# Attention turned around: 128 rows of x on the partitions, probabilities turned by DMA

## The reference

```python
Sim = (e @ w1)[:, :, None] + (ctx @ w2)[:, None, :] + einsum('bid,bjd->bij', e * w3, ctx) + b
A = softmax(Sim, axis=2);  hq = einsum('bij,bjd->bid', A, ctx)
Batt = softmax(max(Sim, axis=2), axis=1);  hc = einsum('bi,bid->bd', Batt, e)
x = x + tanh(g_x) * (concat([e, hq, e * hq, e * hc]) @ W_qv + b_qv)      # e = layernorm(x)
x = x + tanh(g_f) * top2_of_8_experts(layernorm(x))                      # gelu(x @ w1) @ w2
```

## Time and profile before

| | us |
|---|---|
| time, median of 3 runs (lowest, highest) | 2335.67 (2333.89, 2336.94) |
| time of the profiled execution | 2335.5 |
| its span, first to last instruction | 2333.8 |
| PE busy in the span | 2220.5 (95%) |
| DVE, ACT, POOL busy | 1631.7, 1139.5, 144.6 |
| mean granted clock of PE | 0.985 |

### The profile page before, as it was taken

The page is one execution under the profiler, slowest core; times in us unless marked ns, Lnnn a source line. Parts: engine busy times, 40 slices in busy tenths (PEclk is TensorE's granted clock), DMA queues, the critical chain, the costliest instruction groups (busy, mean ns, idle before and its releaser), DMA issues.

```text
span 2333.8 us, 46974 instructions
## 1 busy us (share of the span) xinstructions
PE 2220.5 (95%) x16817; PEld 1607.4 (69%) x16817; DVE 1631.7 (70%) x3445; ACT 1139.5 (49%) x1607; POOL 144.6 (6%) x143
## 2 busy tenths in 40 slices
PE   5899999999999999999879998599999999999997
PEld 4788888888888888888634544456564655656463
DVE  7688888888888888887856678546554555646450
ACT  6565555544555554555633334336362534546260
POOL 0000000000000000000002222101101010100101
PEclk9999999999999999999999999799999999999999
DMA  7811110011111001101355553333435333333411
GB/s 211 251 28 47 45 45 27 18 45 45 45 45 45 18 27 45 45 27 43 148 200 199 213 184 119 103 104 86 109 124 135 113 99 103 90 103 90 132 61 22
DMA packets 164944, 212.31 MB, mean 91 GB/s; under 512 B 106148, under 2 KB 106276, under 8 KB 156700
## 3 DMA queue, kind: packets, MB, share of 16 engines
q1 hardware_dynamic: 154012, 191.13, 24.9%
q0 software_dynamic: 10880, 20.52, 4.5%
HBM read 123.66 MB, written 71.52 MB: 84 GB/s over the span
## 4 chain that ended last, share of the span: by engine, by line
PE 75%; DVE 13%; ACT 4%; issue 4%; DMA 1%; DVEq 1%; ACTq 0%; POOL 0%; another core or an unknown queue 0%; SPq 0%; POOLq 0%
PE ps L1275 20%; PE ps L1951 18%; PE ps L1966 18%; PE ps L1288 12%; PE ps L1701 5%; DVE arena L828 1%; DVE arena L727 1%; DVE arena L725 1%; ACT arena L1150 1%; DVE arena L822 1%; DVE arena L750 1%; DVE arena L815 1%; DVE arena L734 1%; ACT arena L1147 1%; DVE arena L1530 0%
## 5 line engine op out<-in xcount | busy, mean ns | idle before, releaser
L1275 PE MATMUL ps<-arena 128*128 128x256 f16 x4800 | 555.8, 274 | 25.1 <-DMA arena<-arena 9.9
L1288 PE MATMUL ps<-arena 128*128 (+1 forms) x4864 | 561.0, 273 | 7.3 <-DVE arena L822 7.3
L1275 PEld LDWEIGHTS ps<-arena 128*128 128x128 f16 x4800 | 470.1, 98 | 89.4 <-issue 16.6
L1288 PEld LDWEIGHTS ps<-arena 128*128 128x128 f16 x4864 | 475.2, 98 | 68.0 <-DVE arena L822 7.0
L1951 PE MATMUL ps<-arena 128*128 128x320 f16 x3072 | 421.0, 300 | 17.7 <-DMA arena<-rows 17.7
L1966 PE MATMUL ps<-arena 128*128 128x512 f16 x1920 | 415.7, 379 | 0.0
L1951 PEld LDWEIGHTS ps<-arena 128*128 128x128 f16 x3072 | 301.5, 98 | 136.9 <-issue 17.7
L1966 PEld LDWEIGHTS ps<-arena 128*128 128x128 f16 x1920 | 187.9, 98 | 225.2
L1137 ACT ACTIVATE arena<-ps,arena (+1 forms) x192 | 148.9, 775 | 282.8 <-PE ps L1275 282.8
L1701 PE MATMUL ps<-arena 128*128 128x512 f16 x1080 | 240.4, 380 | 10.6 <-DMA arena<-feats 10.6
L1875 DVE SCALAR_TENSOR_TENSOR arena<-arena 128x640 f16<-128x640 f32 x128 | 113.0, 883 | 136.1 <-ACT arena L1919 136.1
(11 more groups left out here) (249 smaller groups left out, 1821.7 us busy)
## 6 DMA issues: line engine op xcount, KB each, us to landing
arena<-in_L_ffn_w SPq DMA_DIRECT2D x64, 1024.0 KB, 10.0
arena<-feats SPq DMA_DIRECT2D x16, 1536.0 KB
arena<-in_x SPq DMA_DIRECT2D x32, 512.0 KB, 3.9
feats<-arena SPq DMA_DIRECT2D x16, 1024.0 KB, 3.9
rows<-arena SPq DMA_DIRECT2D x1, 10320.0 KB, 32.0
feats<-arena SPq DMA_DIRECT2D x16, 512.0 KB, 3.5
out<-arena SPq DMA_DIRECT2D x16, 512.0 KB, 2.8
arena<-in_L_xattn_W_qv SPq DMA_DIRECT2D x4, 1024.0 KB, 9.6
```

Of the source, the lines that this page charges most:

```text
L1275: mm = pe.matmul(out, ctxT[:, 2 * t + h, s, k, :], query[:, r, k, :], start=(k == 0 and s + r == 0), stop=(k == KD - 1 and s == 1))
L1288: mm = pe.matmul(acc[k], ctxN[:, 2 * t + h, s, k * P:(k + 1) * P], prob[:, bass.ds(a % 3, 1), r, h, :].rearrange("p o i -> p (o i)"), star ...
```

## The change

Attention is laid out the other way around, with rows of x on the partitions in all steps. The unit is 128 rows of x (32 units, two in a block), and ctx is cut in 7 chunks: six of 512 columns and a last one of 130.

- Scores: a 128x128 piece of the turned query is the weights, 512 columns of the turned ctx move past it. A unit takes 72 matmuls of 512 columns and 12 of 130.
- Maxima: DVE reduces each chunk of a row along the free axis (`chunk_max`) and then the 7 numbers (`row_max`). The exponential takes the negated maximum as its bias and sums the row while it goes. Running maximum, subtraction, running sum, the transposes of the maxima and the spreading matmuls are gone, and so are the DVE steps for the 2 tail rows of ctx.
- Products: ctx rows (512 wide, not turned) are the moving operand, and the probabilities are the weights, so these must be turned: for each unit and chunk SP issues a DMA transpose (`turn_p`) out of one of two staging buffers (`stage`) into `PT`. A unit takes 76 matmuls of 512 columns. A unit is multiplied two units after its scores: in half u PE makes scores of unit u and products of unit u-2, chunk by chunk, while ACT and DVE make the probabilities of unit u-1.
- The query rows are split with the rows on the partitions and turned by a DMA transpose (`turn_q`), which takes the place of `turn_e`. Its place in SP's list is written in `body`.
- `feats` is stored with rows of x as rows. The merge in stage 2 loads a block with one DMA transpose out of DRAM (`load_feats`), issued as soon as PE has finished with the block before in that buffer, and ahead of the store; x comes in a DMA of its own.
- The start works on chunks of 4 tiles: ACT sums squares (`squares`), PE adds them over partitions (`sums`), and so on; scores of units 0 and 1 are both made there. The blank rows are written in pieces, in the loop.

The core of the diff, in pieces; `half` and `body` replace `iteration` and the loop over blocks.

```diff
-    def load_block(self, sp, x, feats, b, v):
-        rows = bass.ds(b * 256, 256)
-        sp.dma_start(self.ft[v].rearrange("p f s k i -> p (f s k i)"),
-                     feats[bass.ds(b, 1)].rearrange("o p f c -> (o p) (f c)")).then_inc(self.f_loaded[v], 16)
-        sp.dma_start(self.x2[v], x[rows, :].rearrange("(q p) d -> p q d", p=P)).then_inc(self.x_loaded[v], 16)
+    def load_feats(self, sp, feats, b, v):
+        sp.dma_start_transpose(self.ft[v].rearrange("p f s k i -> p (f s k) i"),
+                               feats[bass.ds(b * 256, 256)].rearrange("i f s d -> i (f s d)"))\
+            .then_inc(self.f_loaded[v], 16)
...
+        def turn_q(u, q):
+            sp.wait_ge(row_step, RK * (u + 1))
+            apart(sp, sp_passed)
+            sp.wait_ge(qk_done, UNIT0 if isinstance(u, int) and u == 2 else NC * (u - 1))
+            apart(sp, sp_passed)
+            sp.dma_start_transpose(qT[:, q], qh[:, q].rearrange("p s d -> p (s d)")).then_inc(q_turned[q], 16)
+        def turn_p(u, c):
+            sp.wait_ge(p_ready, NC * u + c + 1)
+            apart(sp, sp_passed)
+            if not isinstance(u, int) or u:
+                sp.wait_ge(av_done, NC * (u - 1) + c + 1)
+                apart(sp, sp_passed)
+            if c < LAST:
+                sp.dma_start_transpose(PT[:, c], stage[:, c % 2].rearrange("p s j -> p (s j)"))\
+                    .then_inc(pt_turned[c], 16)
+            else:
...
+        def body(b, first=False, last=False, norms=True, loads=True, piece=None):
+            u = 2 * b
+            for c in range(NC):
+                turn_p(u - 1, c)
+                if c == 1 and not first and not last:
+                    turn_q(u + 1, 1)
+                if c == 3 and loads:
+                    if not first:
+                        sp.wait_ge(acc_step, 2 * (u - 2))
+                        apart(sp, sp_passed)
+                    load_x(b + 2)
+                if c == 4 and not first:
+                    store_f(u - 3, 1)
+                if c == 5 and norms:
+                    store_e(b + 1)
+            if piece is not None:
+                blank_rows(*piece)
+            for c in range(NC):
+                if not last:
+                    turn_p(u, c)
+                if c == 4:
+                    store_f(u - 2, 0)
+                if c == 5 and norms:
+                    turn_q(u + 2, 0)
...
-        def subtract(a):
-            dve.tensor_tensor(slot_of(a), slot_of(a), bcast(Mb[:, 0, :], 2), ALU.subtract)\
-               .then_inc(sub_done, 1)
-        def low_and_sum(a, t):
-            dve.wait_ge(hi_done, a + 1)
-            pr = prob[:, bass.ds(a % 3, 1)].rearrange("p o s h i -> p (o s) h i")
-            dve.scalar_tensor_tensor(out=pr[:, 1], in0=slot_of(a), scalar=pscale[:, t:t + 1], in1=pr[:, 0],
-                                     op0=ALU.mult, op1=ALU.subtract).then_inc(p_ready, 1)
-            if t == 0:
-                dve.tensor_copy(L, slot_of(a)).then_inc(slot_free, 1)
-            else:
-                dve.wait_ge(slot_free, SLOTS + a)
-                dve.tensor_tensor(L, L, slot_of(a), ALU.add).then_inc(slot_free, 1)
...
+        def chunk_max(n, par, c):
+            dve.wait_ge(scores_ready, n + 1)
+            dve.tensor_reduce(mxc[:, par, c:c + 1], slot(par, c), AX.X, ALU.max).then_inc(max_done, 1)
+        def row_max(u, par, count):
+            s = Steps(dve, m_step, u, MK)
+            dve.wait_ge(max_done, count)
+            s.link(dve.tensor_reduce(m[:, par:par + 1], mxc[:, par, :], AX.X, ALU.max))
+            s.step(dve.tensor_scalar(neg[:, par:par + 1], m[:, par:par + 1], -1.0, None, ALU.mult))
+        def low(u, par, c):
+            dve.wait_ge(hi_done, NC * u + c + 1)
+            p = slot(par, c)
+            if c < LAST:
+                dve.scalar_tensor_tensor(out=stage[:, c % 2, 1, :], in0=p, scalar=pscale[:, c:c + 1],
+                                         in1=stage[:, c % 2, 0, :], op0=ALU.mult, op1=ALU.subtract)\
+                   .then_inc(p_ready, 1)
...
+        def scores(n, bank, par, c, freed=None):
+            if freed is not None:
+                act.wait_ge(p_ready, freed)
+            w = COLS[c][1] - COLS[c][0]
+            act.activation(slot(par, c), psS[bank][:, 0:w], ACT.Identity, bias=zero[:, 0:1],
+                           scale=sinv[:, c:c + 1]).then_inc(scores_ready, 1)
...
+        def probabilities(u, par, c):
+            p = slot(par, c)
+            if c == 0:
+                act.wait_ge(m_step, MK * (u + 1))
+                if not isinstance(u, int) or u >= 2:
+                    act.wait_ge(l_step, 2 * u - 2)
+            act.activation(p, p, ACT.Exp, bias=neg[:, par:par + 1], accum_out=ls[:, par, c:c + 1])\
+               .then_inc(exp_done, 1)
+            if c < LAST:
+                if c >= 2:
+                    act.wait_ge(pt_turned[c - 2], 16 * (u + 1))
+                elif not isinstance(u, int) or u:
+                    act.wait_ge(pt_turned[c + 4], 16 * u)
+            elif not isinstance(u, int) or u:
+                act.wait_ge(pt_turned[c], 16 * u)
+            act.wait_ge(exp_done, NC * u + c + 1)
+            if c < LAST:
+                act.activation(stage[:, c % 2, 0, :], p, ACT.Identity, bias=zero[:, 0:1], scale=pscale[:, c:c + 1])\
+                   .then_inc(hi_done, 1)
...
+        for t in range(NC):
+            if t + 2 < NC:
+                squares(t + 2)
             if t == 0:
...
+            n = t if t <= LAG else LAG + 2 * (t - LAG)
+            scores(n, n % 4, 0, t)
+            if t == 5:
+                query_high(2, 0, row0, RK * 2 + 2)
+            for p in range(2 * t + 4, min(2 * t + 6, NPAIR)):
+                split_high(p)
+            if t >= LAG:
+                n = LAG + 2 * (t - LAG) + 1
+                scores(n, n % 4, 1, t - LAG)
...
+        def sums(c):
+            pe.wait_ge(c_sum, c + 1)
+            if c >= 2:
+                pe.wait_ge(g_step, GK * (c - 2) + 1)
+            pe.matmul(psN[c % 2][:, c:c + 1], onesf, csum[:, c:c + 1], start=True, stop=True).then_inc(n_done, 1)
...
+        def scores(bank, q, c):
+            a, z = COLS[c]
+            out = psS[bank][:, 0:z - a]
+            for k in range(KD):
+                for s, r in ((0, 0), (0, 1), (1, 0)):
+                    mm = pe.matmul(out, qT[:, q, s * KD + k, :], ctxT[:, r * KD + k, a:z],
+                                   start=(k == 0 and s + r == 0), stop=(k == KD - 1 and s == 1))
+            mm.then_inc(qk_done, 1)
...
+        def products(u, q, c, first=False):
+            pe.wait_ge(pt_turned[c], 16 * (u + 1))
+            if c == 0 and not first:
+                pe.wait_ge(acc_step, 2 * u - 3)
+            a, z = TILES[c]
+            for j in range(a, z):
+                if j == JT - 1:
+                    mm = pe.matmul(psO[q], PTl[:, 2, :], ctxN[:, j, 0, :], start=False, stop=True)
+                    continue
+                for s, r in ((0, 0), (0, 1), (1, 0)):
+                    turned = PT[:, c, s * TC + j - a, :] if c < LAST else PTl[:, s, :]
+                    mm = pe.matmul(psO[q], turned, ctxN[:, j, r, :], start=(j + s + r == 0), stop=False)
+            mm.then_inc(av_done, 1)
+        def half(b, i, first=False, last=False):
+            u = 2 * b + i
+            for c in range(NC):
+                if not last:
+                    if c == 0:
+                        pe.wait_ge(q_turned[i], 16 * b)
+                    pe.wait_ge(scores_ready, NC * u + c - 1)
+                    scores(c % 4, i, c)
+                if first and not i and c == LAST:
+                    pe.wait_ge(c_tail, 1)
...
-                               start=(t + h + s + r == 0), stop=tail)
-            return mm
...
-        def turn_maxima(c):
-            pe.wait_ge(merge_done, c + 1)
-            for q in range(QT):
-                mm = pe.transpose(psC[:, q * P:(q + 1) * P], Mc[:, q * P:(q + 1) * P], identf)
-            mm.then_inc(mT_done, 1)
-        def spread_maxima(c):
-            pe.wait_ge(dg_step, DK * (c + 1))
-            for n in range(2):
-                for q in range(QT):
-                    mm = pe.matmul(psC[:, (n * QT + q) * P:(n * QT + q + 1) * P],
-                                   m2[:, n, q:q + 1].broadcast_to([P, P]), identf, start=True, stop=True)
-            mm.then_inc(mb_done, 1)
...
+        for t in range(NC):
+            if t + 2 < NC:
+                sums(t + 2)
+            if t < 2:
+                for v in range(2):
+                    pe.wait_ge(ct_out[v], 2 * t + 2)
             else:
+                if t < LAST:
+                    n = 2 * TC + t - 2
+                    pe.wait_ge(ct_out[n % 2], n // 2 + 1)
+                pe.wait_ge(ct_turned[t], 16 * (3 if t < LAST else 2))
+            n = t if t <= LAG else LAG + 2 * (t - LAG)
+            if n >= 4:
+                pe.wait_ge(scores_ready, n - 3)
+            scores(n % 4, 0, t)
...
             for v in range(2):
```

(27 more changed lines are left out.)

1221 lines of the change are left out of this document (496 added, 725 removed).

## The result

The changed kernel takes 2386.34 us (median of 4 runs, 2384.24 to 2390.32), the kernel before 2336.31 in the same comparison: ratio 1.0218, 95% interval 1.0200 to 1.0235. That is 50 us slower; 2369 was forecast, with 2333 to 2408 as the range, so the sign holds and the time lies in the range; 17 us are to be explained. The profiled execution took 2390.3 us (span 2388.2), 4 above the median; its span is compared with the 2333.8 of before.

What follows compares the result with a forecast made beforehand. PE, busy 95% of the span, was taken to bound the kernel. From 2335.5 us, attention's loop +35.6, the start +9, the end -6 and stage 2 -5 gave 2369 us, range 2333 to 2408.

Steps and rivals of the forecast that it cites:

- the sign: Whole kernel: the change makes it slower, chance 0.80.
- PE's own gain: Attention's blocks: 65.24 us instead of 68.76, 3.5 us less each, 52 us in 15 blocks, mostly from small matmuls.
- DVE and ACT: Attention's halves of 32.6 us: DVE works 20 us and ACT 19, so neither binds and their work stays hidden.
- The query's transpose: Even units' heads, blocks 2 to 15: PE waits 4.4 us for this DMA, 14 times; odd units cost nothing.
- rival 3: Attention's transposes: the DMA queue becomes the bound and they land later, 2450 us and up; chance 0.05.
- The clock after the wait: Even heads: PE runs slowly behind the wait, adding 1.6 us (0 to 2.0), 6.0 us for each head.
- Block 1: Attention's loop: 6.5 us more, as ACT finishes unit 0's probabilities before copying unit 2's scores and PE waits.
- the loop's +35.6: Attention from block 1's first scores to block 15's end: 1069.1 us against 1033.5, 35.6 us more.
- The start: Up to block 1's first scores: rounds of 8.1 us, 93 us (86 to 104) instead of 83.9, +9 us.
- The end: Attention's end to the end of the merge's first block: 55 us instead of 61.0, -6 us (-12 to +3).
- Stage 2: Merge stage: the earlier turned load comes some 5 us sooner, cutting PE's 10.6 us wait; -5 us (-10 to +5).

Runs made afterwards that it cites:

- e1: Changed kernel with the even unit's query transpose issued ahead of chunk 4's probabilities instead of behind chunk 5's: 2298.03 us.
- e9: On top of e1, each 512-column matmul of attention split into two of 256 columns with the same weights: 2304.19 us.
- e2: Changed kernel with the even unit's query transpose one place later, behind chunk 6's probabilities: 2417.06 us.
- e3: Changed kernel with 16 unread matmuls of 512 columns on PE ahead of its wait for the even unit's query: 2357.6 us.
- e4: Changed kernel with PE's sum for chunk t+2 behind the scores of chunk t in the start, instead of ahead: 2374.61 us.
- e6: Changed kernel with 12 unread matmuls of 512 columns on PE behind the scores of chunks 1, 2 and 3 in the start: 2380.68 us.
- e5: Changed kernel with the merge's four 1 MB weight loads behind unit 31's transposes of chunks 1 to 4, one each: 2371.71 us.
- e7: Changed kernel with stage 2's turned load of features issued behind the block's store instead of ahead of it: 2384.57 us.
- e10: Changed kernel with stage 2's turned load behind the store and the wait for the router's steps, as in the kernel before: 2381.94 us.

## Why the prediction was right, and where its steps were off

**PE's own gain.** Right. The block without waits is 65.25 us in e1 (65.24 worked out), 12 matmuls of 130 columns take 0.68 us, and of the 3.5 us a block the width is 0.73 (e9), and the rest goes to the small matmuls and the 0.49 us wait that are gone.

**DVE and ACT.** Right. In e1's window they are busy 59% and 59% of the time, where 20 and 19 of 32.6 us (61 and 58%) were worked out, and PE, busy for all of its 200 us, waits for neither.

**The query's transpose.** Right in place, count, size and cause: 14 waits, 4.4 us each between the starts of matmuls as forecast (4.2 of them idle), at even heads only, moved by e1 and e2 as an order of SP's list should move them. The landing of 3.3 us from the earlier trace rows held beside seven more transposes a unit (3.1 in the median); rival 3, the queue as the bound, is out. By the prediction's estimate from the Trainium skill (Advanced Engine Details and Errata, X-Bar Transpose (TRN2), which puts such transposes at the speed of plain DMAs) the wait would have been 3.3 us; the trace has 1.24 us of issue for each and a wait of 4.4, and decides against it.

**The clock after the wait.** Right in kind and mis-sized: 1.6 us was taken, e3 measures 2.05, and PE's timeline has 2.1 (2.4 and 1.7 in turn). With it the even head costs 71.70 - 65.25 = 6.45 us and not 6.0, which is +6 in 14 heads.

**Block 1.** Of the 6.5 us extra, 2.0 were there. Block 1 took 71.55 us with the wait at block 2's head; in it ACT made PE wait 1.86 us ahead of 115.98 and no more. The timeline of ACT shows why: it needed 16.8 us for unit 0's probabilities and the copies among them, about what was forecast, but began them at 98.39, between its last copies of unit 1's scores and 5.2 us before PE's first scores of block 1. The overlap was wrong and not the cost. This error of -4.5 hid most of the +6 of the clock, and so it is partly luck that the loop's +35.6 met +37.1.

**The start.** The step that failed. The round was worked out right as a chain (e4 takes it apart, and e6's round of 8.0 us is the 8.1 that was summed, whose terms add to 8.0), but with PE's scores at 2.6 us. They take 5.1, at the lower clock, where PE idles over 4 us in each round, and in a chain this is added in full. The three rounds behind the first take 10.75, 10.76 and 10.43 us and not 8.1, 7.6 us more; the first takes 14.8 and not 13. So chunk 4's scores start at 76.5 and not at 68. From there to block 1 it is 27.1 us and not 21: 3.3 are waits that were not in the sum, 2.03 for the transpose of ctx's last chunk and 1.26 for ACT, and 3.0 are scores of PE at the lower clock. That is 14.6 us beyond the 89 of the sum. The prediction had seen the idle time and put 4 us for it at the end, instead of into each round, and 10.6 stay. In the six other traces with the same start, block 1's first scores stand 0.2 to 3.3 us earlier.

**The end.** -6 was forecast and +2.5 came. The sum itself held: 55 us were worked out, and e5 has 54.7 (39.0 to the merge's start, where 38 were summed). What it left out is the place of the merge's weights: it took unit 31's transposes at the pace of the earlier trace rows, and they stood behind 4 MB in the same queue. The order of SP's list, which had been read closely for the query, was not read here.

**Stage 2.** -5 forecast and -4.8 measured, but for a wrong reason, and so by luck. The early place of the turned load removed PE's wait, as forecast, and the time was lost again at the end of the stage; e7 and e10 have the gain without it. What does give it, features stored sooner behind the merge's start, is argued and not shown.

In the profiled spans the start is 10.7 us over its forecast, the end 8.5, the loop 1.5 and stage 2 0.2, 21 in all; 4 of them are the distance of the profiled execution from the median, and 17 are left between 2369 and 2386.

## What to carry to other kernels

Walk down the DMA queue's list for every transfer that someone waits for, and count what stands ahead of it there: two places in SP's list and one in PE's decided between 2% slower and 2.6% faster. In a chain that leaves PE idle, put the slow clock into each of PE's links, not once at the end. And a wait that goes away at the start of a stage is worth something only if its end is not set by another engine or transfer.

## What the hardware showed

Idle matmuls whose result nobody reads made the kernel faster (e3: 3.45 us of them ahead of each wait, 28.7 us less in all), and the loss that they avoid was 2.05 us for each wait, hardly larger behind 6.3 us of idle time (2.2, e2) than behind 4.2 (2.1). Seven transposes of 256 KB a unit in one queue, at a DMA share of 0.44, still landed 3.1 us after their issue in the median (e1); one that was queued behind 4 MB of plain loads took 13.4.
